# First layer on x computed jointly for two tiles from rounded parts, with new orders on every engine

## What is computed

```python
scores = x @ x.T / sqrt(256);  h = softmax(scores) @ x          # inside a segment
bound = circ_conv(layernorm(h), bind_key)                        # binding
hologram = decay_matrix @ bound                                  # running sum over a batch's rows
h = h + x_ln + gate * circ_corr(hologram, unbind_key)
xf = layernorm(h)
logits = gelu(xf @ router_w1 + b) @ router_w2 + b;  two of 8 experts, softmax weights
integrated, v = xf, 0
for _ in range(2):                                               # ITERS = 2
    ctx = concat(integrated, v)                                  # 512 wide
    shared = gelu(ctx @ shared_w1 + b) @ shared_w2 + b           # 64 hidden units, 768 out
    expert[e] = gelu(ctx @ expert_w1[e] + b) @ expert_w2[e] + b  # 8 experts of 64 hidden units
    # each control -> (a, b, g): sigmoid, softplus, sigmoid, new integrated and v
    # mixed by the weights, and by halt = sigmoid(gelu(integrated @ halt_w1) @ halt_w2)
refined = gelu(integrated @ refine_w1 + b) @ refine_w2 + b       # 512 hidden units
out = h + xf + integration_weight * refined
```

## Time and profile before

| | |
|---|---|
| runs, us | 790.24, 790.74, 827.2 (median 790.74) |
| profiled execution, us | 790.91 |
| its span, first to last instruction, us | 789.1 |
| PE busy | 740.8 (94%), 4736 products |
| DVE busy | 652.3 (83%) |
| ACT busy | 525.7 (67%) |
| POOL busy | 290.2 (37%) |
| mean granted clock of TensorE | 0.974 |

### The profile page before, as it was taken

The page is one execution under the profiler, slowest core; times in us unless marked ns, Lnnn a source line. Parts: engine busy times, 40 slices in busy tenths (PEclk is TensorE's granted clock), DMA queues, the critical chain, the costliest instruction groups (busy, mean ns, idle before and its releaser), DMA issues.

```text
span 789.1 us, 14516 instructions
## 1 busy us (share of the span) xinstructions
PE 740.8 (94%) x4736; PEld 645.8 (82%) x4736; DVE 652.3 (83%) x1516; ACT 525.7 (67%) x1308; POOL 290.2 (37%) x393
## 2 busy tenths in 40 slices
PE   4878999999999999999999999999999999999995
PEld 3657888888888888888888888888888888888884
DVE  3655888888888989889889889888888898898864
ACT  4455577567667676686675685776676766766654
POOL 1334423343343252353344334333432532533321
PEclk9578999999999999999999999999999999999999
DMA  8300000000000000000000000000000000000000
GB/s 332 108 14 7 2 1 21 1 21 21 1 21 21 2 21 5 16 22 1 21 21 2 21 22 0 22 21 1 22 21 1 8 8 1 9 1 7 8 1 21
DMA packets 11611, 17.28 MB, mean 22 GB/s; under 512 B 1232, under 2 KB 10504, under 8 KB 11024
## 3 DMA queue, kind: packets, MB, share of 16 engines
q1 hardware_dynamic: 11536, 16.35, 6.1%
HBM read 13.20 MB, written 3.15 MB: 21 GB/s over the span
## 4 chain that ended last, share of the span: by engine, by line
PE 42%; ACT 24%; DVE 22%; issue 9%; POOL 1%; DMA 1%; SPq 0%; POOLq 0%; ACTq 0%; DVEq 0%
PE ctl L474 10%; PE ctl L490 8%; PE ctl L451 5%; ACT L813 4%; ACT L923 4%; ACT L824 3%; ACT ge L846 3%; DVE hm_hi L1087 3%; PE pb L451 3%; PE ctl L493 3%; ACT work L816 2%; ACT work L820 2%; DVE tied L1258 2%; DVE both L1284 2%; DVE gl L1101 2%
## 5 line engine op out<-in xcount | busy, mean ns | idle before, releaser
L366 POOL TENSOR_TENSOR hm_lo<-gl,mexp 128x256 fp32r<-128x256 f32 x144 | 111.3, 799 | 335.2 <-DVE gl L1101 335.2
L474 PE MATMUL ctl<-w2e_hi,hm_hi 128*128 128x512 f32 (+1 forms) x432 | 161.0, 382 | 9.5 <-DVE hm_hi L1087 9.2
L474 PE MATMUL ctl<-w2e_lo,hm_hi 128*128 128x512 f32 (+1 forms) x432 | 149.9, 361 | 0.0
L864 ACT ACTIVATE work<-ctl 128x256 f32<-128x256 f32 (+1 forms) x144 | 70.7, 491 | 91.1 <-PE ctl L493 91.1
L474 PEld LDWEIGHTS ctl<-w2e_hi,hm_hi 128*128 128x128 f32 x432 | 82.4, 191 | 27.0 <-DVE hm_hi L1087 15.5
L490 PE MATMUL ctl<-w2e_hi,hm_lo 128*128 128x512 f32 (+1 forms) x432 | 102.0, 362 | 0.1
L1087 DVE TENSOR_TENSOR hm_hi<-ge,mexp 128x256 fp32r<-128x256 f32 x144 | 79.3, 577 | 22.1 <-ACT ge L846 15.8
L474 PEld LDWEIGHTS ctl<-w2e_lo,hm_hi 128*128 128x128 f32 x432 | 82.6, 191 | 11.2
L451 PEld LDWEIGHTS pa<-x1T,par 128*128 128x128 f32 x768 | 89.4, 192 | 1.1
L451 PE MATMUL pa<-x1T,par 128*128 128x128 f32 x768 | 89.6, 275 | 0.0
L490 PEld LDWEIGHTS ctl<-w2e_hi,hm_lo 128*128 128x128 f32 x432 | 74.5, 188 | 14.7 <-POOL hm_lo L366 0.8
(11 more groups left out here) (174 smaller groups left out, 1741.9 us busy)
## 6 DMA issues: line engine op xcount, KB each, us to landing
work<-params_dram SPq DMA_DIRECT2D x3, 1152.0 KB, 10.1
xT<-turned_dram SPq DMA_DIRECT2D x24, 128.0 KB, 2.3
out_dram<-y SPq DMA_DIRECT2D x24, 128.0 KB, 1.7
xa<-x_dram SPq DMA_DIRECT2D x16, 128.0 KB, 2.3
par<-params_dram SPq DMA_DIRECT2D x1, 1280.0 KB, 12.7
work<-params_dram SPq DMA_DIRECT2D x2, 512.0 KB, 11.0
xa<-x_dram SPq DMA_DIRECT2D x8, 119.0 KB
par<-params_dram SPq DMA_DIRECT2D x1, 512.0 KB, 15.7
```

Of the source, the lines that this page charges most:

```text
L366: TT(hm[1][:, j, c, :], gl[:, c, :], pairs(tile, j, c), ALU.mult).then_inc(done, 1)
L474: mm(dst[:, a:z], hm[0][:, j, c, :], w2e[i][:, c, a:z], start=(c == 0 and i == 0), stop=False)
L864: AF(tan[tile.s][:, 1:kinds, j, :], ctl_t[:, D:kinds * D].rearrange("p (a d) -> p a d", a=kinds - 1), ACT.Tanh, scale=0.5)
```

## The change

- **First layer.** New tensors: `w1e_x`, `w1s_x` (the x half of the first-layer weights, as a rounded part and the rounded rest, made once: the copy on ACT, the subtraction on DVE) and `xj` (x of two tiles side by side, tile n in columns 0 to 127, tile f in columns 128 to 255, again as two parts: the rounded copy on ACT from PSUM, `state_hi`, the rest on POOL, `state_lo`). `first_layer` computes for both tiles at once high by high, low by high and high by low, 256 columns each; the v half of tile n stays fp32, 128 columns, between them. Where only one tile exists, the fp32 form stays. `pb` holds both tiles' shared units side by side, and `pa` and `pc` the experts' (two chunks of 256 columns each). `ge`, `gh` and `gl` get a dimension for the two tiles; a gelu takes both tiles, 256 columns.
- **Attention a slot sooner.** Exponential, its transpose, the product with x, the scaling (now on ACT) and the statistics up to xn are done for e = t+2 rather than in f's slot, whose work begins with the transpose of xn.
- **Orders.** Every engine's `slot` is written in a new order. On ACT all first-layer gelus stand behind the three table loads. On DVE, `weighted` stands ahead of xf. The mask of the first pass for t is half made in the slot before.
- **Start.** The binding matrix's first half is computed behind the first tile's attention product; the parameters with w1 are loaded ahead of w2e; `branch_rates`, `routed_weight` and the parts of w1 are placed in the first slots.
- **End.** The last tile's refine is rounded in halves, its low part on DVE (`last_refine_lo`).

The core of the diff:

```diff
+            def first_layer(dst, wx, w, chunks, n, f, joint, width):
+                x = sides(n, f)
+                for c in chunks:
+                    at = (c % 2) * width if width < 512 else 0
+                    if not (n and f):
...
+                    a, b = at + x.start * P, at + x.stop * P
+                    for i, (g, s) in enumerate(((0, 0), (1, 0), (0, 1))):
+                        if s:
+                            for q in range(KD):
+                                mm(dst[:, at:at + P], w[:, KD + q, c, :], x1T[:, KD + q, :], start=False, stop=False)
+                        if s and c == 0:
+                            passed(pe, x1l_g, joint.at(-2))
+                            passed(pe, xfl_g, joint)
+                        for q in range(KD):
+                            last = mm(dst[:, a:b], wx[g][:, q, c, :], xj[s][:, q, x, :],
+                                      start=(i == 0 and q == 0), stop=(s == 1 and q == KD - 1))
+                return last
...
+            def state_lo(tile, part, src, hi_sb, done, joint):
+                passed(pool, hi_sb, tile)
+                passed(pool, e_ps, joint, back=1, per=2)
+                TT(xj[1][:, :, part, :], src[:, 0:KD, :], xj[0][:, :, part, :].bitcast(fp32),
+                   ALU.subtract).then_inc(done, 1)
...
+            def state_hi(part, src, tile, done, joint):
+                passed(act, e_ps, joint, back=1, per=2)
+                AF(xj[0][:, :, part, :], src[:, 0:D].rearrange("p (k m) -> p k m", k=KD), ACT.Copy).then_inc(done, 1)
```

ACT's slot in the part that the prediction speaks of:

```diff
...
-                if n.exists() and t.exists():
-                    shared_units(n, s2_ps, s2_sb, sh2, sab2, halt2_ps, sl2_v)
...
+                    state(xfT, pd, D, f, xfT_ps, xfT_sb)
+                    state_hi(1, pd, f, xfh_sb, f)
+                    passed(act, rh_ps, f)
+                    AF(rh[:, :], pd[0:HID, 0:P], ACT.Gelu, bias=pv("b1r", HID)).then_inc(rh_sb, 1)
...
                     unit(t, 2, u1_sb, u1_ps, ctl[0], 2)
...
+                    state(x1T, pc, 2 * D, n, x1T_ps, x1T_sb)
+                    if f.exists():
+                        state_hi(0, pc, n, x1h_sb, f)
...
+                        nc.scalar.preload_act_table_set("exp_and_others")
+                        softmaxed(e)
                     softplus_of(m, t)
                     table_of_gelus()
...
+                    shared_units(n, 0, s2_sb, sh2, sab2, halt2_ps, sl2_v, f)
...
+                    expert_units(n.exists(), f.exists(), f)
```

More of the change, by code:

```diff
@@ new lines, in slot @@
+                if f.exists():
+                    if f.low == 0:
+                        pe.wait_ge(set_act, 2)
+                    passed(pe, mask_v, f)
+                    if e.exists():
+                        passed(pe, eT_sb, e)
+                    else:
+                        passed(pe, e_sb, f, per=2)
+                    for j in range(2):
+                        last = mm(pc[0:MR, j * P:(j + 1) * P], mask[:, j, 0:MR], identb[:, :], start=True, stop=True)
+                    last.then_inc(mT_ps, 1)
@@ L741, in slot @@
-                if n.exists():
-                    passed(pe, hm2_v, n, per=3)
-                    passed(pe, u2_sb, n, per=BR, step=1)
-                    for a, b in spans(3 * D):
-                        expert_hi(ctl[1], 1, n, hm2_v, a, b)
-                if t.newest():
-                    passed(pe, e2_sb, n, per=2)
-                    hidden(pa, P, w1e, range(EC), x1T, 2 * KD, e2_ps)
-                    passed(pe, x1T_sb, t)
+                    joint_experts(True, False, f.at(1))
@@ L751, in slot @@
+                    passed(pe, e_sb, f.at(1), per=2)
                     second_turned(m)
                 if f.exists():
[L754 to L761 removed]
+                    passed(pe, mT_sb, f)
@@ L763, in slot @@
+                    if e.exists():
+                        passed(pe, h_sb, e)
+                    else:
+                        passed(pe, mask_v, f)
+                    both = maskT[:, :, :].rearrange("e j m -> e (j m)")
+                    for c in range(EC):
+                        last = mm(cd[:, 2 * c * P:2 * (c + 1) * P], expandb[:, c, :], both, start=True, stop=True)
+                        if c % 2:
+                            last.then_inc(me_ps, 1)
                 if n.exists():
@@ L1079, in shared_lo, with mask_hi @@
                 V.tensor_tensor(sab[HID:P, 0, :], sh[0:HID, :], sab[0:HID, 0, :].bitcast(fp32), ALU.subtract).then_inc(done, 1)
-            def mask_hi(tile, j, e_sb, done, read, back):
+            def mask_hi(tile, j, part, joint, done, read, back):
                 passed(dve, read, tile, back=back, per=BR, step=j + 2)
@@ L1187, in slot @@
-                if m.exists() and not last_in:
-                    gates(m)
                 if f.exists():
```

765 lines of the change are left out of this document (433 added, 332 removed).

## The result

| | runs | median, us | span of the profiled execution | mean granted clock |
|---|---|---|---|---|
| before | 8 | 790.18 (787.44 to 827.2) | 789.1 | 0.974 |
| after | 8 | 783.81 (782.25 to 786.07) | 784.1 | 0.972 |

The ratio is 0.9928, 95% interval 0.9915 to 0.9941: 0.7% faster, a third of what was forecast (771, 2.5%). Inside a band of 2% this is no change; the interval, which leaves out the one disturbed run of 827.2, says it is a small gain. The time lies in the range 757 to 786 and in rival B's 779 to 790, but not by B's mechanism, as the stages show. That it is inside the range is no confirmation: the term for the start came out with the wrong sign, outside its own bounds, and the range was wide enough to hold it.

A forecast was written before the change was run, and what follows sets the result against it. PE was taken as the bound, with the ring through DVE and ACT barely shorter. Span 789.1 - 15 (22 slots) - 4 (start) - 1 (end) = 769.1, 771 as measured time; range 757 to 786.

The forecast's parts named there:

- rival B: Steady slots: the ring through DVE and ACT gives the saving back as PE waits of 1.3 to 1.6; 779 to 790; chance 0.22.
- First layer on x: Joint first layer per slot: 20 fp32 products, 4.46 us, become 30 instructions of 256 columns, 3.60; saves 0.86.
- Four waits: Four tight places where PE waits under the new orders; 0.75 to 1.15 us a slot, taken as 0.8.
- the second: Wait before the router's second product, for the gelu rh on ACT and two handovers; PE waits 0.35 us.
- the changes between rounded and fp32 products: Two more switches per first-layer chunk; nothing added, 0.3 us a slot kept as upper bound.
- item 1: Wait before the transposes of xf: PE has 7.4 to 7.9 us of work, DVE needs 8.1; PE waits 0.3.
- C: Slower: POOL's two new subtractions hold DVE operations; one hold of 0.9 gives a 30.6 us slot and 787; chance 0.05.
- A: PE is fed: waits shrink to 0 to 0.5 us a slot, slot 28.9 to 29.4, 752 to 763; chance 0.25.
- 22 slots: Slots where both tiles exist, each going from 30.42 to 29.7 us; together they bring 15 us.
- Start: First slots: first tile's attention is scaled about 5 us sooner, less one-off work; gain 4 us, bounds 0 and 7.
- End: Last tile's low part in halves on DVE, rounding overlapping the gelus; gain 1 us, bounds 0 and 2.
- Faster by over 2%: Whole kernel below 775 us: the forecast's lower two thirds plus all of A; chance 0.60.

The follow-up runs named there:

- e1: The after kernel with the x half of the first layer as fp32 products of 128 columns per tile; 792.17 us, ratio 1.0031 to before.
- e11: The after kernel with ACT's second-pass softplus done for 8 of 256 columns; 770.6 us, ratio 0.9753 to before.
- e4: The after kernel with POOL's new subtractions for x's low part cut to 8 of 128 columns; 784.43 us, ratio 0.9928 to before.
- e14: The after kernel with 24 unread PE products in the 3.17 us pause before the last but one refine step; 784.23 us, ratio 0.9915 to before.
- e5: The after kernel with 16 unread PE products in each of slots 1 and 2, where the refine step will be; 781.9 us, ratio 0.9882 to before.
- e9: The after kernel with the second and third tiles' attention pulled ahead of and into the first layer; 778.95 us, ratio 0.9857 to before.
- experiment 6: Two runs on slot 0's start: e9, and e2 with the first tile's one-off work rearranged, the latter 783.48 us, ratio 0.9915 to before.
- e2: The after kernel with POOL's two one-off operations on the refine weights made ahead of the router's chain; 782.68 us, ratio 0.9895 to before.
- e13: e9 plus 16 unread PE products in each of slots 1 and 2 and 24 in the tail's 3.2 us pause; 775.45 us, ratio 0.9806 to before.

## Why the prediction was off, point by point

**First layer on x: right.** 0.86 a slot forecast, 0.91 measured by e1 against after. The joint groups start 0.12 apart, as the row at 449.28 said, and not the 0.109 by the formula of the Trainium skill (TensorE: Matmul & The Clock Gate, Back-to-back issue gap).

**Four waits: three of four right in place, the slot right by luck.** For the four named places 0.8 was forecast and some 0.85 measured; but the second stands before the transposes of x1, for DVE held by POOL, and not before the router's second product. With two places that weren't named all waits come to 1.1. Against them the sum set 0.63, which was idle time, where before really waited about 1.0. The two errors, 0.3 and 0.4, all but cancel, so a slot of 29.80 for 29.7 doesn't confirm the terms. With the measured ones, 30.42 - 0.91 - 1.0 + 1.1 = 29.6, and no run says where the 0.2 that is missing goes; the changes between rounded and fp32 products, which the prediction put at nothing with 0.3 as a bound, are one place for it. In item 1 the terms listed for PE add up to 7.05 and not to 7.4 (the transposes of x2 are missing); the trace has some 7.65. Rival B's mechanism is there, through ACT's stretch of tables (e11), and it takes half of the layer's saving, not all of it. C's holds don't come from the new subtractions (e4), but a steady slot has one of 0.97 us on x1, and PE waits 0.25 behind it. C's own sum was off as well: a slot of 30.6 is 4 us over 22 slots more than now, so 790 and not 787; and A counts 6 us for a start and an end that are 5.

**22 slots: the smaller step that failed.** The sum gave the steady saving to 22 slots. 19 had it, and the stretch 22 to 23 brought 1.8. The slots 1 and 2 have a first layer for two tiles but not yet a refine step, and the wait that forecast item 1 put at 0.3 is there 2.0, because the 1.8 us of the refine layer that the item counted as PE's cover is missing. Behind it the granted clock fell. Forecast for the two was 63.11 - 1.4 = 61.7. They took 65.59 in after's trace, 3.9 more, but 62.16 in e14's, 0.5 more, by the same pauses. So most of the miss here goes with the clock behind the pause and differs from execution to execution; e5, with products alone, has 60.54.

**Start: the step that failed most.** The first tile's attention came 5.9 us sooner, as worked out (9.00 for "near 9.5"), and the conclusion "4 us" didn't follow. The working followed the first tile only. The same edit moves the second tile's attention into the slot before, "leaves slot 0 as well", and there it is the last thing that slot 0's start waits for; I had booked it as relief. Slot 0 starts 1.6 later, not 4 sooner, and nothing shows for certain why: e9's trace has DVE's one-off work and ACT's copy of w2a in the way (experiment 6), and no run takes both away. The stretch 0 to 1 adds 3.3. Taking the third tile's attention ahead gives 4.4 back (e9), freeing xn of POOL's 2.35 gives 1.75 (e2); the two aren't independent. Together that is 4.9 us lost where 4 were forecast as a gain, 8.9 of the 15 us between the forecast span and the measured one. I had named "the low part of r2 on POOL" as something against the 4, without asking what DVE would do beside it, though rival C had the mechanism for the steady slot. The first slot's masked products, forecast for 57, came at 62.55, against 62.01 before.

**End: right in the last tile, lost again in the tail.** From the last refine step to the end before took 8.7 us and after 8.06: the halves on DVE saved 0.6 of the forecast 1. The tail as a whole is 1.2 longer, at a clock of 0.95 (0.97 before), and e13 shows the same instructions at 1.00 in 61.07 with 24 added. So the term was right for the last tile, and is smaller than what the clock and the moved waits take or give in the tail.

**Chances.** Faster by over 2% had 0.60. Its support was a steady term of 15 us that proved right to 1.5; nearly all of the miss is in the start and the end, given as -4 and -1 with bounds of 0, which were +4.9 by slot 1 and +1.2, and in the slots 1 and 2 (3.9 in this trace, 0.5 in another). A loss at the start was left out of the bounds without a reason.

## What to carry to other kernels

A pipeline's fill slots are not steady slots with less in them: where a stage is missing, its work is missing as cover, so every wait in the sum has to be taken again there, with the next tile's path and not only the first one's. A pause of PE can cost what follows it, at the lower clock; 16 products that nobody reads in each of two pauses of 2 us went with 1.6 to 5.05 us less over two slots, by which unchanged trace one compares, and 24 in another pause with a tail shorter by 3.2 (64.3 in e9, 61.1 in e13) or not shorter at all (e14). So compare a stage with the same stage of a second trace in which it wasn't changed, before a difference in it is called the work of an edit. Read PE's waits from start to start: its idle time hides those under 0.2 us.

## What the runs showed of the hardware that I had not expected

The recorded duration of a product reaches about 0.17 past the next start, so 0.85 us of waiting a slot appears as nearly none (534.05 busy of 536.51). An elementwise operation of DVE beside POOL's 128x1024 took 2.43 us instead of 0.41, and in every slot with a refine step one beside POOL's 128x512 takes 1.39 instead of 0.42. The granted clock of the same tail was 0.95 or 1.00 with the same instructions in it, and that is 2.4 us of 63.5 (e14 and e13), more than several of the edits tried here; slots 1 and 2 differ by 3.4 us in the same way (after and e14).
